# Head-compact recurrent weights: the key side as two 64-row matmuls per product, into two PSUM banks

## The chip, the core and the metric

The kernel runs on one core of one Trainium2 chip. TensorE (PE; its weight loads are shown as PEld) multiplies, VectorE (DVE), ScalarE (ACT) and GpSimd (POOL) do the elementwise work, SyncE (SP) moves tiles. The metric is the device time of one execution in microseconds. Everything is fp32. In the trace one fp32 matmul of the kernel shows as two PE instructions, one PE transpose as one.

## The reference, cut to what matters

The layer is a test-time-training attention over 2048 tokens, a windowed softmax attention and a mixture of experts with 32 experts, added to the input. The part that the change touches is the recurrence: four heads of size 64, 16 chunks of 128 tokens, and three weight matrices per head that change from chunk to chunk:

```
def step(carry, xi):
    W0, W1, W2, M0, M1, M2 = carry
    qi, ki, vi, l0, l1, l2, mi = xi
    hid = einsum('bcd,bhd->bch', qi, W2)
    gate = silu(einsum('bcd,bhd->bch', qi, W0))
    out = einsum('bch,boh->bco', gate * hid, W1)
    gba = einsum('bcd,bhd->bch', ki, W0)
    hbm = einsum('bcd,bhd->bch', ki, W2)
    sg = silu(gba); hidden = sg * hbm
    dhidden = einsum('bco,boh->bch', vi, W1)
    dhbm = dhidden * sg
    dgba = silu_bp(dhidden * hbm, gba)
    dw1 = einsum('bco,bch->boh', vi, hidden * l1)
    dw0 = einsum('bch,bcd->bhd', dgba, ki * l0)
    dw2 = einsum('bch,bcd->bhd', dhbm, ki * l2)
    # dw += momentum * mean; five Newton-Schulz steps; W = renorm(W + dw)
    ...
```

## The kernel before

The four heads are held as two groups (g = 0, 1) of two heads (h = 0, 1): head h of a group sits on partitions 64h to 64h+63. The 16 chunks are unrolled. Each of the 15 first chunks ends in a boundary, at which the weights of the next chunk become ready; the last chunk has no weight update.

Each engine runs one instruction list in an order written out by hand (`body` and its `fill` tables); semaphores join the lists. The pieces around the change are these.

- `renorm(m)` (DVE, L1175) writes the new weights `Wn[g]`, for group 0 and then group 1.
- `turn_w(m, g)` (PE, L736) turns `Wn[g]` with three PE transposes of 128 x 64 into `CA[g]`, on partitions 0 to 63. `w_T` (ACT) copies the result with two activations, one per head, into `WT[g]`, a 128 x 3 x 128 tile whose 64 x 64 blocks on the diagonal hold the turned weights of the two heads and whose other blocks stay zero.
- `w_bd(m)` (DVE, L1186 and L1187) copies the two blocks of W1 into the block-diagonal `W1BD[g]`: four copies of 64 x 64 for both groups, right behind `renorm`. Behind it stand `total`, `weights` and, in the next body, `ln_stats`.
- `k_side(i, g)` (PE) makes, for 128 tokens and both heads at once, one matmul of 256 moving columns against `WT` (W0 and W2) and one of 128 against `W1BD`, into one bank, `CB[g]`. ACT's `k_side` reads that bank (sigmoid of 128 columns, copy of 256 columns into `ks`), DVE's `k_side` (L1075 to L1094) makes the twelve elementwise steps of the gradient, POOL's `k_u` (L333) one product of it.
- `q_side(i)` (PE) makes four matmuls of 128 x 128 x 128 with `WT`, and `q_out(i)` two more with the W1 part of `WT`, which is block-diagonal.
- On DVE, `q_gate` (L1193, L1195) follows `k_side`, then `grad` (momentum, squares, row sums), then `sum_copy` and `x_first`. On PE, `grads(i, 0)` and `grads(i, 1)` wait for `dga`, then come `h_up(i, 2)`, half of `shared_up` (which waits for `gh` of `q_gate`), `sums` (waits for the row sums of `grad`), the other half of `shared_up`, `h_up(i, 3)` and the first turn of X (`ns_turn`, L699).
- On POOL, `k_u(i, 0)`, `k_u(i, 1)` and `h_sq(i, 1)` (L363, the square of 128 x 512) follow one another.

The names L426 (ACT) and L629 (PE matmul) are helper lines that many steps share; tiles tell them apart.

Of the kernel before, what the change touches and what calls it, by code (L numbers as in the profile page):

```python
# [27 lines left out]
ALU = mybir.AluOpType  # L28
ACT = mybir.ActivationFunctionType
# [3 lines left out]
P = 128  # L33
D = 256
KT = D // P
HD = 64
NH = 4
G = 2
# [9 lines left out]
W0, W2, W1 = range(3)  # L48
# [25 lines left out]
def build(nc, x, wall_d, rows_d, wo, fast_d, affine_d, fc1T, fc2T, e1T, e2T, upT, downT, ident_d, fixed_d, out):  # L74
# [3 lines left out]
    with ExitStack() as ctx:  # L78
        def sb(name, shape):
            return ctx.enter_context(nc.sbuf_tensor(name, shape, F32))  # L80

        def bank(name):
            return ctx.enter_context(nc.psum_tensor(name, [P, 512], F32))
# [13 lines left out]
        ident = sb("ident", [P, P])  # L97
# [10 lines left out]
        bias, gb, og_s = rows[:, 0:SMALL], rows[:, SMALL:SMALL + E], rows[:, SMALL + E:SMALL + E + HD]  # L108

        Wn = [sb(f"Wn{g}", [P, 3, HD]) for g in range(G)]  # L110
        W1BD = [sb(f"W1BD{g}", [P, P]) for g in range(G)]
        WT = [sb(f"WT{g}", [P, 3, P]) for g in range(G)]
        Mom = [sb(f"Mom{g}", [P, 3, HD]) for g in range(G)]
        nrm = [sb(f"nrm{g}", [P, 3]) for g in range(G)]

# [7 lines left out]
        ks = [sb(f"ks{g}", [P, 3, P]) for g in range(G)]  # L123
# [28 lines left out]
        vT = sb("vT", [P, G, P])  # L152
# [44 lines left out]
        CC = [ctx.enter_context(nc.psum_tensor(f"CC{g}", [P, 1024], F32)) for g in range(G)]  # L197
        CA = [CC[g][:, 0:512] for g in range(G)]
        CB = [CC[g][:, 512:1024] for g in range(G)]
        M0 = bank("M0")  # L200
        M1 = bank("M1")
        HB = bank("HB")
# [3 lines left out]
        def per_group(name):  # L206
            return [sem(f"{name}{g}") for g in range(G)]
# [13 lines left out]
        e_dw, e_G, e_s3, e_ssb, e_sst, e_pw, e_x = (per_group(n) for n in ("dw", "G", "s3", "ssb", "sst", "pw", "X"))  # L221
        e_ax, e_t, e_xt, e_am = (per_group(n) for n in ("aX", "turn", "XT", "Am"))
        e_prod, e_mp = (per_group(n) for n in ("product", "Mp"))
        e_up, e_rn, e_rp, e_wn, e_bd, e_wt, e_WT = (per_group(n) for n in ("upd", "rn", "rp", "Wn", "W1BD", "wt", "WT"))
        e_qs, e_gsig, e_gt1, e_gh, e_qo, e_to = (sem(n) for n in ("q_side", "gate_sig", "gt1", "gh", "q_out", "to_copied"))
        e_msq, e_rms, e_tf, e_ttt = (sem(n) for n in ("ms", "rms", "ttt_steps", "ttt_ready"))
        e_at, e_aT, e_win, e_as, e_sm, e_nb, e_pr = (sem(n) for n in ("raw_turned", "aT", "window", "scores", "masked", "negmax", "probs"))
# [187 lines left out]
        def _(act):  # L415
# [9 lines left out]
            def a(out_, in_, func, **kw):  # L425
                return nc.scalar.activation(out_, in_, func, **kw)  # L426
# [43 lines left out]

            def k_side(i, g):
                act.wait_ge(e_k[g], i + 1)
                a(ks[g][:, 0, :], CB[g][:, 0:P], ACT.Sigmoid)
                a(ks[g][:, 1:3, :].rearrange("p w c -> p (w c)"), CB[g][:, P:3 * P], ACT.Copy).then_inc(e_kc[g], 1)

            def xt(i, g, it):
                act.wait_ge(e_t[g], NI * i + it + 1)
# [2 lines left out]
            def w_T(m, g):  # L480

                act.wait_ge(e_wt[g], m + 1)
                for h in range(2):
                    c = slice(h * HD, (h + 1) * HD)
                    ins = a(WT[g][c, :, c], CA[g][0:HD, 0:3 * P].rearrange("p (w c) -> p w c", w=3)[:, :, c], ACT.Copy)
                ins.then_inc(e_WT[g], 1)

            def gate_sig(i):
                act.wait_ge(e_qs, i + 1)
# [127 lines left out]
        def _(pe):  # L617
# [10 lines left out]
            def mm(out_, lhsT, rhs, start=True, stop=True):  # L628
                return pe.matmul(out_, lhsT, rhs, start=start, stop=stop)  # L629
# [43 lines left out]
            def k_side(i, g):  # L673

                pe.wait_ge(e_qkT, i + 1)
                pe.wait_ge(e_vT, i + 1)
                pe.wait_ge(e_WT[g], i + 1)
                mm(CB[g][:, 0:2 * P], qkT[:, 2 + g, :], WT[g][:, W0:W2 + 1, :].rearrange("p w c -> p (w c)"))
                pe.wait_ge(e_bd[g], i + 1)
                mm(CB[g][:, 2 * P:3 * P], vT[:, g, :], W1BD[g][:, :]).then_inc(e_k[g], 1)  # L680

            def grads(i, g):
                if g == 0:
# [42 lines left out]
            def turn_w(m, g):  # L726

                if isinstance(m, int):
                    if m == 0:
                        pe.wait_ge(e_ttw, 16 * G)  # L730
                    else:
                        pe.wait_ge(e_wn[g], m)
                else:
                    wn_in[g].wait()
                for w in range(3):
                    ins = pe.transpose(CA[g][0:HD, w * P:(w + 1) * P], Wn[g][:, w, :], ident[:, :])  # L736
                ins.then_inc(e_wt[g], 1)


            def q_side(i):  # L740

                pe.wait_ge(e_ot, i)
                for g in range(G):
                    pe.wait_ge(e_WT[g], i + 1)
                pe.wait_ge(e_qkT, i + 1)
                for g in range(G):
                    for n, w in enumerate((W0, W2)):
                        ins = mm(M0[:, (2 * g + n) * P:(2 * g + n + 1) * P], WT[g][:, w, :], qkT[:, g, :])
                ins.then_inc(e_qs, 1)

            def q_out(i):
                pe.wait_ge(e_gh, i + 1)
                pe.wait_ge(e_aT, i + 1)
                for g in range(G):
                    ins = mm(M1[:, g * P:(g + 1) * P], gh[:, g, :], WT[g][:, W1, :])
                ins.then_inc(e_qo, 1)


# [209 lines left out]
        def _(dve):  # L968
# [7 lines left out]
            nc.vector.memset(vw[:, 1, :], 0.0)  # L976
            for g in range(G):
                nc.vector.memset(Mom[g][:, :, :], 0.0)
                nc.vector.memset(W1BD[g][:, :], 0.0)
                nc.vector.memset(WT[g][:, :, :], 0.0)  # L980
            nc.vector.memset(lt[:, :, :], 0.0).then_inc(e_init, 1)

            aggr_in = Expect(dve, e_stats, "aggr_in")
# [83 lines left out]
            def k_side(i):  # L1067


                tt, stt = nc.vector.tensor_tensor, nc.vector.scalar_tensor_tensor  # L1070
                sg, hbm, dhi = ([ks[g][:, n, :] for g in range(G)] for n in range(3))

                def silu(g):
                    dve.wait_ge(e_kc[g], i + 1)
                    tt(kt[g][:, 0, :], CB[g][:, 0:P], sg[g], ALU.mult).then_inc(e_kd[g], 1)  # L1075

                def slope(g):
                    dve.wait_ge(e_kd[g], 3 * i + 1)
                    stt(kt[g][:, 1, :], sg[g], 1.0, kt[g][:, 0, :], ALU.subtract, ALU.mult).then_inc(e_kd[g], 1)

                def derivative(g):
                    dve.wait_ge(e_kd[g], 3 * i + 2)
                    tt(kt[g][:, 2, :], sg[g], kt[g][:, 1, :], ALU.subtract).then_inc(e_kd[g], 1)

                def through(g):
                    dve.wait_ge(e_kd[g], 3 * i + 3)
                    dve.wait_ge(e_ku[g], i + 1)
                    tt(dga[g][:, :], kt[g][:, 2, :], kt[g][:, 3, :], ALU.mult).then_inc(e_dgr[g], 1)

                def hidden(g):  # L1090
                    tt(hid[g][:, :], kt[g][:, 0, :], hbm[g], ALU.mult)

                def dhidden(g):
                    tt(dhb[g][:, :], kt[g][:, 0, :], dhi[g], ALU.mult)  # L1094

                for step, g in ((silu, 0), (slope, 0), (hidden, 0), (silu, 1), (derivative, 0), (dhidden, 0), (slope, 1),
                                (through, 0), (hidden, 1), (derivative, 1), (dhidden, 1), (through, 1)):
                    step(g)
# [77 lines left out]
                                                      nrm[g][:, w:w + 1], ALU.mult, ALU.mult)  # L1176
                    ins.then_inc(e_wn[g], 1)

            def w_bd(m):

                for g in range(G):
                    if isinstance(m, int) and m == 0:
                        dve.wait_ge(e_ttw, 16 * G)
                    else:
                        dve.wait_ge(e_wn[g], m)
                    nc.vector.tensor_copy(W1BD[g][0:HD, 0:HD], Wn[g][0:HD, W1, :])  # L1186
                    nc.vector.tensor_copy(W1BD[g][HD:P, HD:P], Wn[g][HD:P, W1, :]).then_inc(e_bd[g], 1)  # L1187


            def q_gate(i):  # L1190
                dve.wait_ge(e_gsig, i + 1)
                v = M0[:, :].rearrange("p (g w t) -> p g w t", g=G, w=2)
                nc.vector.tensor_tensor(gt1[:, :, :], v[:, :, 0, :], gsig[:, :, :], ALU.mult).then_inc(e_gt1, 1)  # L1193
                dve.wait_ge(e_gt1, i + 1)
                nc.vector.tensor_tensor(gh[:, :, :], v[:, :, 1, :], gt1[:, :, :], ALU.mult).then_inc(e_gh, 1)  # L1195
# [146 lines left out]

            def body(i, last):
                if last:
                    q_gate(i)
                    att_scale(i)
                    y_acc(i, 1)
                    q_ms(i)
                    y_acc(i, 2)
                    att_mask(i)  # L1350
                    att_max(i)
                    y_acc(i, 3)
                    q_norm(i)
                    y_acc(i, 4)
                    att_out(i)
                    for u in range(5, NU):
                        y_acc(i, u)
                    y_sum(i)
                    total(i)
                    return  # L1360
                m = i + 1
                ln_stats(m)
                k_side(i)
                q_gate(i)
                grad(i)
                sum_copy(i, 0)
# [19 lines left out]
                update(i)  # L1386
                y_sum(i)
                renorm(m)
                w_bd(m)
                total(i)  # L1390
                weights(m)

# [6 lines left out]
            for g in range(G):  # L1399
                dve.wait_ge(e_rp[g], 1)  # L1400
                nc.vector.tensor_copy(nrm[g][:, :], r3[g][:, 4, :]).then_inc(e_up[g], 2)
            w_bd(0)
            dve.wait_ge(e_const, 16 * NCONST)
            prep_z(0)
            prep_silu_qk(0)
# [48 lines left out]
```

## Time and profile before

| | |
|---|---|
| median of 3 runs | 830.14 us (828.5 to 830.5) |
| profiled execution, its own time | 830.14 us |
| its span in the profile | 828.1 us |
| granted TensorE clock, mean | 0.996 of full speed |
| PE matmul busy | 780.7 us (94%) |
| DVE busy | 714.6 us (86%) |
| ACT busy | 354.0 us (43%) |
| POOL busy | 406.8 us (49%) |

The 2.0 us between the span and the execution's own time lie outside the profile. Busy shares are averages over the whole span. One chunk takes 51.34 us: the wait of POOL for the row sums at a boundary ends at 382.93 us in one chunk and at 434.27 us in the next, and the fifteen boundaries look alike. The boundary between 382 and 398 us of the span is the one read below.

### The profile page before, as it was taken

What the parts mean: (1) busy time and instruction counts of PE and PEld (TensorE: products, weight loads), DVE (VectorE), ACT (ScalarE), POOL (GpSimd) and SP (SyncE); (2) the same over time, 40 slices, a digit from 0 to 9 for tenths busy, and PEclk for the clock granted to TensorE, in tenths of its full rate; (3) what the DMA queues carried; (4) which work ended last, traced back from release to release, by engine and by line L of the source; (5) the groups of instructions that cost most, each with busy time, mean ns of one, the idle gap of its engine ahead of it and who ended that gap; (6) DMA issues with size and microseconds to landing.
All of it is one profiled execution on the core that took longest, in us unless ns stands there. A gap on an engine that the chain in (4) does not pass through costs nothing.

```text
span 828.1 us, 24889 instructions
## 1 busy us (share of the span) xinstructions
PE 780.7 (94%) x9776; PEld 668.5 (81%) x9776; DVE 714.6 (86%) x2592; ACT 354.0 (43%) x868; POOL 406.8 (49%) x535
## 2 busy tenths in 40 slices
PE   3899999999999999999999999999999999999997
PEld 1888888888888888878888788887888888888886
DVE  4789898898988979889798897988979889898876
ACT  2544344443444434444344444444444444434533
POOL 1654555445454454544555445544465444655442
PEclk9899999999999999999999999999999999999999
DMA  8100000000000000000000000000000000000000
GB/s 321 54 3 14 9 2 21 3 13 9 2 21 2 14 8 2 21 2 15 8 3 20 2 15 9 3 21 2 15 8 2 21 2 15 8 2 15 2 15 7
DMA packets 9811, 15.09 MB, mean 18 GB/s; under 512 B 1120, under 2 KB 8928, under 8 KB 9440
## 3 DMA queue, kind: packets, MB, share of 16 engines
q1 hardware_dynamic: 7904, 7.80, 3.2%
q10 hardware_dynamic: 1792, 5.70, 1.8%
q8 instruction: 78, 1.28, 0.6%
q14 instruction: 37, 0.30, 0.1%
HBM read 11.41 MB, written 2.10 MB: 16 GB/s over the span
## 4 chain that ended last, share of the span: by engine, by line
PE 53%; DVE 33%; issue 6%; ACT 5%; POOL 2%; DMA 1%; SPq 0%; DVEq 0%
PE CC L629 18%; PE M L629 13%; PE HB L629 8%; DVE acc L1328 8%; PE YB L629 8%; DVE Wn L1175 4%; DVE Mp L1138 2%; DVE dhb L1094 2%; DVE X L1146 2%; PE CC L699 2%; DVE Am L1131 2%; POOL r L285 2%; DVE sm L1233 1%; DMA rows<-in_rows 1%; PE CC L700 1%
## 5 line engine op out<-in xcount | busy, mean ns | idle before, releaser
L363 POOL TENSOR_TENSOR hq<-hr 128x512 f32<-128x512 f32 x128 | 137.1, 1071 | 71.9 <-ACT hr L426 71.9
L285 POOL TENSOR_TENSOR r<-r,half 128x3 f32<-128x3 f32 (+1 forms) x78 | 77.9, 1011 | 155.1 <-DVE r L1116 67.9
L629 PE MATMUL HB<-xlT,e_s 128*128 128x128 f32 x1024 | 143.0, 283 | 0.4 <-ACT xlT L426 0.4
L629 PE MATMUL YB<-e_s,hq 128*128 128x128 f32 x1024 | 141.3, 281 | 1.8 <-DVE acc L1328 0.8
L629 PEld LDWEIGHTS HB<-xlT,e_s 128*128 128x128 f32 x1024 | 126.7, 193 | 6.8 <-ACT xlT L426 0.7
L1328 DVE SCALAR_TENSOR_TENSOR acc<-YB,cw,acc 128x128 f32<-128x128 f32 x448 | 125.4, 342 | 7.9 <-PE YB L629 7.9
L341 POOL TENSOR_TENSOR aX<-X,a_tile 128x192 f32<-128x192 f32 x150 | 92.9, 640 | 79.9 <-DVE X L1146 79.9
L426 ACT ACTIVATE hr<-HB 128x512 f32<-128x512 f32 x128 | 76.1, 594 | 128.5 <-PE HB L629 128.5
L629 PEld LDWEIGHTS YB<-e_s,hq 128*128 128x128 f32 x1024 | 124.2, 191 | 7.4 <-issue 4.1
L629 PEld LDWEIGHTS CC<-X,Mp 64*64 64x64 f32 x1800 | 58.3, 135 | 23.6 <-issue 11.3
L629 PEld LDWEIGHTS CC<-Am 64*64 64x64 f32 x1800 | 59.5, 134 | 21.8 <-DVE Am L1131 18.2
L426 ACT ACTIVATE XT<-CC 128x256 f32<-128x256 f32 x150 | 50.8, 381 | 59.7 <-PE CC L700 59.5
L629 PE MATMUL CC<-X,Mp 64*64 64x64 f32 x1800 | 68.6, 222 | 7.6 <-DVE Mp L1138 7.6
L629 PE MATMUL CC<-Am 64*64 64x64 f32 x1800 | 69.8, 223 | 1.9
L1146 DVE SCALAR_TENSOR_TENSOR X<-CC,aX 128x192 f32<-128x192 f32 x150 | 51.3, 352 | 13.4 <-PE CC L629 13.3
L629 PE MATMUL M<-wall,xnT 128*128 128x512 f32 (+1 forms) x128 | 56.9, 551 | 3.6 <-DMA rows<-in_rows 3.6
L629 PEld LDWEIGHTS CC<-XT 64*64 64x64 f32 x1800 | 43.2, 133 | 20.7 <-ACT XT L426 14.7
L1131 DVE COPY Am<-CC 128x192 f32<-128x192 f32 x150 | 48.4, 347 | 9.3 <-PE CC L629 8.3
L1138 DVE SCALAR_TENSOR_TENSOR Mp<-Am,CC 128x192 f32<-128x192 f32 x150 | 49.8, 351 | 7.2 <-PE CC L629 3.6
L629 PE MATMUL CC<-XT 64*64 64x64 f32 x1800 | 55.6, 232 | 0.0
L699 PE MATMUL CC<-ident,X 128*64 128x128 f32 x150 | 39.7, 281 | 0.0
L333 POOL TENSOR_TENSOR kt<-ks 128x128 f32<-128x128 f32 x30 | 13.7, 459 | 51.0 <-ACT ks L426 51.0
(180 smaller groups left out, 1525.3 us busy)
## 6 DMA issues: line engine op xcount, KB each, us to landing
xa<-in_x SPq DMA_DIRECT2D x16, 128.0 KB, 2.1
e_s<-in_e1T ACTq DMA_DIRECT2D x1, 2048.0 KB, 12.7
e_s<-in_e2T ACTq DMA_DIRECT2D x1, 2048.0 KB, 19.3
xr<-in_x SPq DMA_DIRECT2D x16, 128.0 KB, 2.2
out<-ot SPq DMA_DIRECT2D x16, 128.0 KB, 1.7
wall<-in_wall SPq DMA_DIRECT2D x1, 820.0 KB, 7.1
up_s<-in_upT ACTq DMA_DIRECT2D x1, 512.0 KB, 15.9
down_s<-in_downT ACTq DMA_DIRECT2D x1, 512.0 KB, 20.0
```

Of the source, the lines that this page charges most:

```text
L285: return pool.tensor_tensor(dst, src, expo[:, 0:n], ALU.pow)
L341: pool.tensor_tensor(aX[g][:, :, :].rearrange("p w c -> p (w c)"), X[g][:, :, :].rearrange("p w c -> p (w c)"), a_tile[:, it, :], ALU.mult ...
L363: pool.tensor_tensor(hq[b][:, :, :], hr[b][:, :, :], hr[b][:, :, :], ALU.mult).then_inc(e_hq, 1)
L426: return nc.scalar.activation(out_, in_, func, **kw)
L629: return pe.matmul(out_, lhsT, rhs, start=start, stop=stop)
L699: pe.transpose(CA[g][0:HD, 0:P], X[g][:, 0, :], ident[:, :])
L1094: tt(dhb[g][:, :], kt[g][:, 0, :], dhi[g], ALU.mult)
L1131: nc.vector.tensor_copy(Am[g][:, :, :], CC[g][:, 0:6 * P].rearrange("p (w c) -> p w c", w=3)[:, :, 0:HD])\
L1138: nc.vector.scalar_tensor_tensor(Mp[g][:, :, :].rearrange("p w c -> p (w c)"), Am[g][:, :, :].rearrange("p w c -> p (w c)"), b / c, CA[g][ ...
L1146: nc.vector.scalar_tensor_tensor(X[g][:, :, :].rearrange("p w c -> p (w c)"), CB[g][:, 0:3 * HD], NS[it][2], aX[g][:, :, :].rearrange("p w ...
L1175: ins = nc.vector.tensor_scalar(Wn[g][:, w, :], Wn[g][:, w, :], r3[g][:, 5, w:w + 1], nrm[g][:, w:w + 1], ALU.mult, ALU.mult)
L1328: ins = nc.vector.scalar_tensor_tensor(acc[:, e, :], y, w, acc[:, e, :], ALU.mult, ALU.add)
```

## The change

The turned weights are kept compact: `WT[g]` becomes 128 x 3 x 64, head h on its own 64 partitions, without zeros.

- `turn_w` makes six matmuls of 64 x 64 x 64 against the identity, each on its head's partitions, in place of three transposes. `w_T` becomes one activation of 128 x 192.
- `k_side` on PE makes, per head, one matmul with 64 rows of contraction and 128 moving columns (W0 and W2), head 0 into `CA[g]` and head 1 into `CB[g]`, and then one per head with 64 moving columns for W1, which it takes straight from `Wn`. `KS[g]` is a view of both banks, through which ACT's and DVE's steps read.
- `q_side` makes eight matmuls of 64 x 64 with 128 moving columns in place of four full ones.
- `w_bd` is gone. A new `w_out(i)` on DVE writes the block-diagonal `WO[g]` (for `q_out`) from `WT`, with four copies of the same shape; it stands behind DVE's `k_side` and before `q_gate`.
- At the start the memsets of `W1BD` and of `WT` (two of 128 x 384) are replaced by one of `WO` per group.

```diff
         Wn = [sb(f"Wn{g}", [P, 3, HD]) for g in range(G)]
-        W1BD = [sb(f"W1BD{g}", [P, P]) for g in range(G)]
-        WT = [sb(f"WT{g}", [P, 3, P]) for g in range(G)]
+        WT = [sb(f"WT{g}", [P, 3, HD]) for g in range(G)]
+        WO = [sb(f"WO{g}", [P, P]) for g in range(G)]
...
+        KS = [CC[g][:, :].rearrange("p (h c) -> p h c", h=2)[:, :, 0:3 * HD] for g in range(G)]
...
             def k_side(i, g):
                 act.wait_ge(e_k[g], i + 1)
-                a(ks[g][:, 0, :], CB[g][:, 0:P], ACT.Sigmoid)
-                a(ks[g][:, 1:3, :].rearrange("p w c -> p (w c)"), CB[g][:, P:3 * P], ACT.Copy).then_inc(e_kc[g], 1)
+                a(ks[g][:, 0, :].rearrange("p (h c) -> p h c", h=2), KS[g][:, :, 0:HD], ACT.Sigmoid)
+                a(ks[g][:, 1:3, :].rearrange("p w (h c) -> p h w c", h=2),
+                  KS[g][:, :, HD:3 * HD].rearrange("p h (w c) -> p h w c", w=2), ACT.Copy).then_inc(e_kc[g], 1)
...
                 act.wait_ge(e_wt[g], m + 1)
-                for h in range(2):
-                    c = slice(h * HD, (h + 1) * HD)
-                    ins = a(WT[g][c, :, c], CA[g][0:HD, 0:3 * P].rearrange("p (w c) -> p w c", w=3)[:, :, c], ACT.Copy)
-                ins.then_inc(e_WT[g], 1)
+                a(WT[g][:, :, :].rearrange("p w c -> p (w c)"), CA[g][:, 0:3 * HD], ACT.Copy).then_inc(e_WT[g], 1)
...
                 pe.wait_ge(e_WT[g], i + 1)
-                mm(CB[g][:, 0:2 * P], qkT[:, 2 + g, :], WT[g][:, W0:W2 + 1, :].rearrange("p w c -> p (w c)"))
-                pe.wait_ge(e_bd[g], i + 1)
-                mm(CB[g][:, 2 * P:3 * P], vT[:, g, :], W1BD[g][:, :]).then_inc(e_k[g], 1)
+                halves = [(slice(h * HD, (h + 1) * HD), (CA, CB)[h][g]) for h in range(2)]
+                for c, dst in halves:
+                    mm(dst[:, 0:2 * HD], qkT[c, 2 + g, :], WT[g][c, W0:W2 + 1, :].rearrange("p w c -> p (w c)"))
+                for c, dst in halves:
+                    ins = mm(dst[:, 2 * HD:3 * HD], vT[c, g, :], Wn[g][c, W1, :])
+                ins.then_inc(e_k[g], 1)
...
                 for w in range(3):
-                    ins = pe.transpose(CA[g][0:HD, w * P:(w + 1) * P], Wn[g][:, w, :], ident[:, :])
+                    for h in range(2):
+                        c = slice(h * HD, (h + 1) * HD)
+                        ins = mm(CA[g][c, w * HD:(w + 1) * HD], Wn[g][c, w, :], ident[c, c])
                 ins.then_inc(e_wt[g], 1)
...
                     for n, w in enumerate((W0, W2)):
-                        ins = mm(M0[:, (2 * g + n) * P:(2 * g + n + 1) * P], WT[g][:, w, :], qkT[:, g, :])
+                        for h in range(2):
+                            c = slice(h * HD, (h + 1) * HD)
+                            ins = mm(M0[c, (2 * g + n) * P:(2 * g + n + 1) * P], WT[g][c, w, :], qkT[c, g, :])
...
-                    ins = mm(M1[:, g * P:(g + 1) * P], gh[:, g, :], WT[g][:, W1, :])
+                    pe.wait_ge(e_wo[g], i + 1)
+                    ins = mm(M1[:, g * P:(g + 1) * P], gh[:, g, :], WO[g][:, :])
...
-                nc.vector.memset(W1BD[g][:, :], 0.0)
-                nc.vector.memset(WT[g][:, :, :], 0.0)
+                nc.vector.memset(WO[g][:, :], 0.0)
...
-            def w_bd(m):
-
-                for g in range(G):
-                    if isinstance(m, int) and m == 0:
-                        dve.wait_ge(e_ttw, 16 * G)
-                    else:
-                        dve.wait_ge(e_wn[g], m)
-                    nc.vector.tensor_copy(W1BD[g][0:HD, 0:HD], Wn[g][0:HD, W1, :])
-                    nc.vector.tensor_copy(W1BD[g][HD:P, HD:P], Wn[g][HD:P, W1, :]).then_inc(e_bd[g], 1)
+            def w_out(i):
+
+                for g in range(G):
+                    dve.wait_ge(e_WT[g], i + 1)
+                    nc.vector.tensor_copy(WO[g][0:HD, 0:HD], WT[g][0:HD, W1, :])
+                    nc.vector.tensor_copy(WO[g][HD:P, HD:P], WT[g][HD:P, W1, :]).then_inc(e_wo[g], 1)
...
                 if last:
+                    w_out(i)
                     q_gate(i)
...
                 k_side(i)
+                w_out(i)
                 q_gate(i)
...
                 renorm(m)
-                w_bd(m)
                 total(i)
```

## Rows read from the trace of the kernel before

**Rows 1.** The page: busy time by engine, shares of the chain by engine.
```profile
PE 780.7 (94%) x9776; PEld 668.5 (81%) x9776; DVE 714.6 (86%) x2592; ACT 354.0 (43%) x868; POOL 406.8 (49%) x535
...
PE 53%; DVE 33%; issue 6%; ACT 5%; POOL 2%; DMA 1%; SPq 0%; DVEq 0%
```
**Rows 2.** The chain at one boundary, in order of time: start, us, what.
```profile
388.20 0.91 PE CC L629 x4
389.13 0.56 ACT ks L426 x2
...
390.29 1.12 DVE dhb L1094
...
392.68 0.73 PE CC L629 x12
```
**Rows 3.** The timeline from the new weights to DVE's key side: start, us, engine, line, operation, [idle before, releaser].
```profile
386.71 0.18 DVE L1186 COPY W1BD<-Wn 64x64 f32<-64x64 f32 x1
386.85 0.52 PE L736 MATMUL CC<-ident,Wn 128*64 128x128 f32 x3
...
387.32 0.19 DVE L1187 COPY W1BD<-Wn 64x64 f32<-64x64 f32 x1
387.40 0.66 ACT L426 ACTIVATE WT<-CC 64x192 f32<-64x192 f32 x2 [0.43 <-PE CC L736]
...
387.63 0.39 PE L629 MATMUL CC<-W1BD,vT 128*128 128x128 f32 x2
...
388.77 0.28 DVE L1075 TENSOR_TENSOR kt<-CC,ks 128x128 f32<-128x128 f32 x1
```
**Rows 4.** The timeline from there to the first turn of X.
```profile
389.76 0.46 POOL L333 TENSOR_TENSOR kt<-ks 128x128 f32<-128x128 f32 x1 [0.59 <-ACT ks L426]
...
389.92 0.44 DVE L1083 TENSOR_TENSOR kt<-ks,kt 128x128 f32<-128x128 f32 x1
...
390.17 1.09 POOL L363 TENSOR_TENSOR hq<-hr 128x512 f32<-128x512 f32 x1
...
391.96 0.30 PE L629 MATMUL CC<-kl,dga 128*64 128x64 f32 x2 [0.64 <-DVE dga L1088]
...
392.34 0.28 DVE L1088 TENSOR_TENSOR dga<-kt 128x128 f32<-128x128 f32 x1
...
392.99 0.42 DVE L1195 TENSOR_TENSOR gh<-M,gt 128x256 f32<-128x256 f32 x1
...
393.33 0.73 DVE L1105 SCALAR_TENSOR_TENSOR Mom<-Mom,mmc,CC 128x192 f32<-128x192 f32 x2
...
394.51 0.60 DVE L1112 TENSOR_REDUCE r<-sq 128x3 f32<-128x192 f32 x2
...
395.12 0.53 PEld L629 LDWEIGHTS CC<-r,fixed 128*128 128x128 f32 x4
...
397.08 0.36 DVE L1126 TENSOR_TENSOR X<-Mom,r 128x192 f32<-128x192 f32 x1
...
397.50 0.30 PE L699 MATMUL CC<-ident,X 128*64 128x128 f32 x1
```
**Rows 5.** Timeline rows of runs of weight loads and matmuls of either size.
```profile
394.22 0.97 PEld L629 LDWEIGHTS M<-xnT,up_s 128*128 128x128 f32 x8
```
```profile
398.95 0.32 PEld L629 LDWEIGHTS CC<-XT 64*64 64x64 f32 x12 [0.17 <-issue]
398.95 0.46 PE L629 MATMUL CC<-XT 64*64 64x64 f32 x12
```
```profile
407.59 0.78 PEld L629 LDWEIGHTS CC<-Am 64*64 64x64 f32 x24 [0.76 <-DVE Am L1131]
```
**Rows 6.** Groups by line and shape, ACT: xcount | busy us, mean ns | idle before.
```profile
L426 ACT ACTIVATE XT<-CC 128x256 f32<-128x256 f32 x150 | 50.8, 381 | 59.7 <-PE CC L700 59.5
...
L426 ACT ACTIVATE ks<-CC 128x128 f32<-128x128 f32 x30 | 8.3, 278 | 7.3 <-PE CC L629 6.9
```
**Rows 7.** The timeline at the start of the program.
```profile
12.09 5.08 PE L629 MATMUL M<-wall,xnT 128*128 128x512 f32 x8 [3.60 <-DMA rows<-in_rows]
```

More of the change, by code:

```diff
@@ L223, in build @@
         e_prod, e_mp = (per_group(n) for n in ("product", "Mp"))
-        e_up, e_rn, e_rp, e_wn, e_bd, e_wt, e_WT = (per_group(n) for n in ("upd", "rn", "rp", "Wn", "W1BD", "wt", "WT"))
+        e_up, e_rn, e_rp, e_wn, e_wo, e_wt, e_WT = (per_group(n) for n in ("upd", "rn", "rp", "Wn", "WO", "wt", "WT"))
         e_qs, e_gsig, e_gt1, e_gh, e_qo, e_to = (sem(n) for n in ("q_side", "gate_sig", "gt1", "gh", "q_out", "to_copied"))
@@ L1074, in silu @@
                     dve.wait_ge(e_kc[g], i + 1)
-                    tt(kt[g][:, 0, :], CB[g][:, 0:P], sg[g], ALU.mult).then_inc(e_kd[g], 1)
+                    tt(kt[g][:, 0, :].rearrange("p (h c) -> p h c", h=2), KS[g][:, :, 0:HD],
+                       sg[g].rearrange("p (h c) -> p h c", h=2), ALU.mult).then_inc(e_kd[g], 1)
                 def slope(g):
@@ L1401, in _ @@
                 nc.vector.tensor_copy(nrm[g][:, :], r3[g][:, 4, :]).then_inc(e_up[g], 2)
-            w_bd(0)
             dve.wait_ge(e_const, 16 * NCONST)
```

## The prediction, made before the changed kernel was run

> **What bounds the kernel now.** I read the page first: PE has 94% matmul busy time and the chain lies 53% on PE and 33% on DVE [rows 1]. So neither engine alone sets the time; they hand a chain to each other, and what counts is which of them is late at each hand-over around the edit. The second view was the chain in order of time at one of the 15 boundaries [rows 2], the third the timeline of all engines over the same stretch [rows 3, 4]. The reader should see four hand-overs.
>
> (a) The weights of group 1 are complete just before PE's turn of them starts, at 386.85; it ends at 387.37, ACT copies them with two activations until 388.06, PE makes `k_side` of group 1 from 388.20 to 389.11, ACT's two activations take 0.56 [rows 2, 3]. So `ks` of group 1 is there at 389.69. The four copies of `w_bd` run beside this on DVE, and DVE's first step on group 0 starts at 388.77 [rows 3].
>
> (b) The next wait is between DVE and POOL. `k_u` of group 1 on POOL starts at 389.76, and `h_sq` behind it ends at 391.26. DVE's `dhb`, a step of the same shape as `dga` (0.28), takes 1.12 and ends at 391.41, 0.15 behind POOL [rows 2, 4]. The derivative step L1083 (0.44) got through between the two POOL instructions.
>
> (c) From there DVE works without a gap: last `dga` at 392.34, ends 392.62; `q_gate` until 393.41 (`gh`: 392.99 + 0.42); momentum, squares and row sums until 395.11 [rows 4]. PE makes `grads(1)` at 392.68, right behind `dga`.
>
> (d) `sums` starts on PE at 395.12. Its data of group 0 was there at 394.87 (the first of the two reductions of 394.51 to 395.11; I read 0.24 back for the second). PE is here the later one, by 0.25. Then X of group 0 is ready at 397.44 and PE turns it at 397.50 [rows 4]: both arrive together, so a delay of `sums` goes through to the Newton-Schulz steps in full.
>
> **The change part by part**, for one boundary.
>
> *Turn.* Three transposes of 0.52 in all [rows 3] become six matmuls, 12 instructions of 64 x 64 x 64. Twelve such instructions take 0.46 from first start to last end [rows 5]. The end moves by -0.06: from 387.37 to 387.31.
>
> *Copy of the turned weights.* Two activations, 0.66 [rows 3], become one of 128 x 192. Between 278 ns for 128 columns and 381 for 256 [rows 6] that is 0.33. `WT` of group 1 is ready at 387.31 + 0.02 + 0.33 = 387.66 instead of 388.06.
>
> *Key side on PE.* Before, a group has 2 instructions of 256 columns and 2 of 128; now 8 instructions with 64 rows: 4 with 128 moving columns and 4 with 64, all with 128 weight columns. The trace has no instruction of 64 rows by 128 columns. The nearest rows give two bounds. If the row halves work side by side as the 64 x 64 quarters do, I scale from these: 12 loads start within 0.32 and 24 within 0.78, so 0.024 to 0.030 each at 64 columns, 0.05 to 0.06 at 128 [rows 5]. If they don't, each costs what a full 128-column load costs, 0.97/8 = 0.12 less overlap, so 0.11 (the next step of PE after these eight loads is 0.90 later) [rows 5]. I take 0.06, since the 64 x 64 products alternate the halves in just this way. Group 0 starts at about 387.25: last start 387.25 + 7 x 0.06 = 387.67, with some 0.23 for the last matmul itself 387.90. Before, its last matmul ended at 387.63 + 0.39 = 388.02 [rows 3]. Group 1 follows without waiting for `WT`, and ends about 388.45, before ACT is done with group 0. ACT then sets the time: `ks` of group 0 at 387.90 + 0.57 = 388.47, of group 1 at 389.04. That is 0.65 earlier than 389.69. I cost the strided reads of the two banks by ACT and DVE at nothing, since the element counts are the same; if each lost 0.05 by it, the gain below would be 0.1 less, which the range holds.
>
> The Trainium skill (TensorE: Matmul & The Clock Gate, section LDWEIGHTS) says that a weight load takes a time given by its columns, whatever its rows, which speaks against halving the rows: eight loads of 128 columns for four. Its section on packing small matmuls says that loads for different row groups overlap with running matmuls. With the first alone the sum would be the rival B below, with both it is my forecast; the trace agrees with the second for 64 x 64 shapes [rows 5] and shows no 64 x 128 shape.
>
> *What DVE makes of the 0.65.* The gain can't pass (b) whole. `h_sq` now ends at about 391.26 - 0.65 = 390.61, but DVE comes to its derivative step, the fifth instruction behind `ks` of group 0, at 388.47 + 4 x 0.28 = 389.6 at the earliest, and at 390.0 if one of the four waits for a `k_u` (0.46). If it reaches the gap between `k_u` and `h_sq` as before, only `dhb` waits, and all is gained: 0.54 to 0.65. If it misses it, the derivative waits behind `h_sq` too, which costs one more step of 0.20 (the pitch of these steps), and leaves about 0.40. I take g = 0.45 for the gain at the last `dga`.
>
> The Trainium skill (SBUF — State Buffer, who interferes with whom) calls this an exclusive lock on a shared pair of ports, taken for a whole instruction. The trace agrees: `dhb` ends 0.15 behind POOL's instruction [rows 4].
>
> *w_bd leaves, w_out comes.* The four copies cost 0.80 at 386.71 to 387.51 [rows 3]. There they are covered: DVE waits for `ks` anyway, so taking them out gives at most the 0.14 by which DVE's first step was later than `ks` of group 0. In the new place, between the last `dga` and `q_gate`, nothing covers them: DVE is busy without a gap from (b) to the row sums. I charge 0.80. Queued behind are `q_gate`, momentum, squares and row sums, and `sums` on PE waits for the last. `gh` would come at 393.41 + 0.80 - g; PE wants it for `shared_up` at 394.22 - g [rows 4, 5], so that wait just doesn't open. PE's `sums` could run at 395.12 - g, its data comes at 394.87 + 0.80 - g. PE waits 0.55. What is left of each boundary is
>
> shift = 0.80 - 0.25 - g = 0.55 - g = +0.10 us.
>
> *q_side.* Eight instructions of 128 x 128 with 128 columns become 16 of 64 x 64 with 128 moving columns. By the pitches above, 16 x 0.055 = 0.9, as before; serial it would be 1.8. PE stands idle for 0.64 before `grads` [rows 4] and comes free up to 0.6 sooner from `k_side`, so even the high bound costs nothing there. `q_out` has the same matmuls and a wait that is long over.
>
> *Start and end.* The memsets and the four copies before the first chunk (some 1.5 us of DVE) lie before 12.09 us, when PE's projection has waited 3.60 us for a DMA [rows 7]: nothing. In the last chunk there is no key side: `w_out` needs only `WT`, and DVE then waits for PE's `q_side` and ACT's gate, so it is covered; uncovered it would cost 0.80 once.
>
> *The sum.* 15 x 0.10 = +1.5 us on the profiled execution's own 830.14, which is also the median: 831.6. With g between 0.40 and 0.65, +2.3 to -1.5.
>
> **The rivals.**
>
> A, the forecast: the halves overlap, the moved copies use up what that gives. 831.6, own range 828.6 to 834.5.
>
> B: the row halves don't overlap. Pitch 0.11: group 0 ends at 387.25 + 0.77 + 0.22 = 388.24, group 1 at 389.12, `ks` of group 1 at 389.69 as before, g = 0. Shift 0.55, +8.3 us: 838.4. For it: eight full-width loads where there were four. Against it: the 64 x 64 rows.
>
> C, faster: the shared port is passed at the best moment and DVE's first step is freed of its 0.14 too. g = 0.65 + 0.14 = 0.79, shift -0.24, -3.6 us: 826.5. It decides as soon as g exceeds 0.55 + 0.17 = 0.72. Against it: DVE would have to find the port free at each of its steps.
>
> D, the port takes more: with `ks` of group 1 close behind that of group 0, POOL's two `k_u` and `h_sq` stand back to back, and two or three DVE steps wait instead of one. g = 0.20, shift 0.35, +5.3 us: 835.4. For it: DVE's step L1083 already stretches to 0.44 behind `k_u` [rows 4].
>
> **How the numbers follow.** A 0.52 (of which 0.46 within 0.3%, that is 2.5 us, about what a measurement of this kernel can tell from no change, and 0.06 above), B 0.18, C 0.12, D 0.18. Faster 0.12, same 0.46, slower 0.42. The prediction is A's. The range from 826.5 to 838.5 holds A, D, C's value and B's at its edge; half of B and half of C may lie outside, 0.15.
>
> **What would show it.** ACT copies `WT` in one piece of 0.33 and starts `ks` of group 1 right behind that of group 0; weight loads of 64 x 128 at a pitch near 0.06; DVE's copies between `dga` and `gt`, 0.80; PE idle for about 0.5 before `sums`, with DVE's reduction as releaser, where it had none. The chunk of 51.34 us becomes 51.4. Wrong would be: loads at 0.11 (B), a `dga` that comes less than 0.3 sooner after the weights (D), no wait before `sums` (C). What would upset all of it is a moved phase between POOL and DVE somewhere in the Newton-Schulz steps, which I assume to keep their pattern.

## The result, and the profile of the changed kernel

The changed kernel takes 834.52 us (median of 5 runs, 833.24 to 834.67) against 830.25 us (5 runs) of the kernel before: 0.51% slower, ratio 1.0051, interval 1.0037 to 1.0066. That is inside the predicted range, 2.9 us above its point of 831.6 and at the upper edge of the narrower range that the prediction gave its own forecast (828.6 to 834.5). The profiled execution took 833.24 us, the shortest of the five, with a span of 831.3.

The page, busy time and the chain by engine. The columns are those of [rows 1].

```profile
PE 789.5 (95%) x10312; PEld 672.7 (81%) x10312; DVE 714.5 (86%) x2590; ACT 344.2 (41%) x836; POOL 408.6 (49%) x535
...
PE 48%; DVE 39%; issue 6%; ACT 4%; POOL 2%; DMA 1%; SPq 0%; DVEq 0%
```

VectorE is as busy as before (714.5 against 714.6 us). Yet its share of the chain rose from 33% to 39%, and PE's fell from 53% to 48%. The same amount of VectorE work now stands in a place where something waits for it; the lines below show which.

The chain at the same boundary, with the wait that ends each chunk's weight update as a clock.

```profile
383.83 0.86 POOL r L286
...
389.00 0.56 ACT ks L427 x2
...
390.82 1.12 DVE dhb L1101
...
393.92 0.44 DVE gt L1197
...
394.38 0.42 DVE gh L1199
394.80 0.65 DVE Mom L1112 x2
...
396.30 0.64 PE CC L628 x4
...
435.45 0.86 POOL r L286
```

This view gives the loss. A chunk takes 435.45 - 383.83 = 51.62 us, where it took 51.34: 0.28 more, and 15 x 0.28 = 4.2 us. The medians differ by 4.27. Before, the chain went from the last `dga` to PE's `grads`; now it stays on VectorE through the gate, momentum and squares. POOL's step starts at 383.83 where it started at 382.93, so 0.90 is taken off the times below to lay them beside [rows 3, 4].

The timeline of the boundary.

```profile
386.94 0.76 DVE L1182 TENSOR_SCALAR Wn<-Wn,r,nrm 128x64 f32<-128x64 f32 x3
...
387.79 0.43 PEld L628 LDWEIGHTS CC<-ident,Wn 64*64 64x64 f32 x12 [0.33 <-DVE Wn L1182]
387.80 0.56 PE L628 MATMUL CC<-ident,Wn 64*64 64x64 f32 x12
...
388.29 0.30 PEld L628 LDWEIGHTS CC<-WT,qkT 64*128 64x128 f32 x4
388.29 0.49 PE L628 MATMUL CC<-WT,qkT 64*128 64x128 f32 x4
...
388.41 0.33 ACT L427 ACTIVATE WT<-CC 128x192 f32<-128x192 f32 x1 [0.79 <-PE CC L628]
388.51 0.31 PEld L628 LDWEIGHTS CC<-Wn,vT 64*128 64x128 f32 x4
388.62 0.34 PE L628 MATMUL CC<-Wn,vT 64*128 64x64 f32 x4
...
388.85 0.33 PEld L628 LDWEIGHTS CC<-WT,qkT 64*128 64x128 f32 x4
388.88 0.49 PE L628 MATMUL CC<-WT,qkT 64*128 64x128 f32 x4
389.00 1.13 ACT L427 ACTIVATE ks<-CC 128x128 f32<-128x128 f32 x4 [0.26 <-PE CC L628]
...
390.56 0.34 DVE L1090 TENSOR_TENSOR kt<-ks,kt 128x128 f32<-128x128 f32 x1
...
390.71 1.09 POOL L364 TENSOR_TENSOR hq<-hr 128x512 f32<-128x512 f32 x1
...
392.50 0.30 PE L628 MATMUL CC<-kl,dga 128*64 128x64 f32 x2 [0.45 <-DVE dga L1095]
...
392.88 0.27 DVE L1095 TENSOR_TENSOR dga<-kt 128x128 f32<-128x128 f32 x1
...
393.08 0.18 DVE L1190 COPY WO<-WT 64x64 f32<-64x64 f32 x1
...
393.70 0.19 DVE L1191 COPY WO<-WT 64x64 f32<-64x64 f32 x1
...
394.87 1.15 PE L628 MATMUL M<-xnT,up_s 128*128 128x128 f32 x8
...
395.91 0.60 DVE L1119 TENSOR_REDUCE r<-sq 128x3 f32<-128x192 f32 x2
...
396.30 0.64 PE L628 MATMUL CC<-r,fixed 128*128 128x3 f32 x4 [0.29 <-DVE r L1119]
...
398.27 0.36 DVE L1133 TENSOR_TENSOR X<-Mom,r 128x192 f32<-128x192 f32 x1
```

The reader should see three things. First, ACT now runs all four activations of `ks` in one piece, 389.00 to 390.13; less 0.90 that ends at 389.23, where it ended at 389.69: 0.46 gained. Second, the last `dga` starts at 391.98 on the old clock, where it started at 392.34: 0.36 of the 0.46 is left. Third, the four copies follow it, and the reductions start at 395.01 on the old clock instead of 394.51: 0.50 late. PE's `sums` says in its bracket that it sat idle for 0.29 until VectorE's reduction. No such wait stood at that place before. X follows, 398.27 - 0.90 = 397.37 against 397.08 [rows 4]: 0.29 late. So 0.21 of the 0.50 was covered.

The start of the program went the other way. PE's projection of the first chunk began earlier:

```profile
10.40 4.29 PE L628 MATMUL M<-wall,xnT 128*128 128x512 f32 x5 [2.52 <-DMA rows<-in_rows]
```

It was 12.09 before [rows 7]. After seven boundaries of +0.28 the clock should be 1.96 late and is only 0.90 late. About 0.6 of that 1.1 us was gained at the start: the last `dga` of the first chunk starts at 31.62 instead of 32.56, which is 0.94 sooner, and 0.36 of this is the gain that every boundary has. Another 0.35 belongs to the kernel before, in whose profiled execution one early chunk took 51.69 us and the others 51.33 to 51.36; the rest is rounding of the 0.28. The profiled execution is also the shortest of its five. Whether the change has part in the earlier start was not tried.

### The profile page after: what moved, and what is told of

It is laid out like the page before. It is cut to its first block, busy times and chain, and to the rows that moved or that the text cites. A ratio compares the mean times of both kernels' runs of the same rounds, so it can differ in the third digit from the quotient of the medians.

```text
span 831.3 us, 25927 instructions
## 1 busy us (share of the span) xinstructions
PE 789.5 (95%) x10312; PEld 672.7 (81%) x10312; DVE 714.5 (86%) x2590; ACT 344.2 (41%) x836; POOL 408.6 (49%) x535
## 4 chain that ended last, share of the span: by engine, by line
PE 48%; DVE 39%; issue 6%; ACT 4%; POOL 2%; DMA 1%; SPq 0%; DVEq 0%
PE CC L628 17%; PE M L628 13%; DVE acc L1332 8%; PE YB L628 8%; PE HB L628 6%; DVE Wn L1182 3%; DVE dhb L1101 2%; DVE Mp L1145 2%; DVE X L1153 2%; PE CC L701 2%; DVE Am L1138 2%; POOL r L286 2%; DVE sm L1237 1%; PE CC L702 1%; DVE r L1243 1%
## 5 line engine op out<-in xcount | busy, mean ns | idle before, releaser
L702 PE MATMUL CC<-ident,X 128*128 128x128 f32 x150 | 38.5, 273 | 0.0
```

The source lines that it names most:

```text
L702: pe.transpose(CA[g][:, P:2 * P], X[g][:, 1:3, :].rearrange("p w c -> p (w c)"), ident[:, :])\
```

## The experiments

Every time is a median, with the ratio to the kernel before, which was run beside it on the same chip (830.99 us for the first four, 830.79 for the last four). The recorded expectations speak of theories. Theory 1: the moved copies stand on a stretch of VectorE without a gap. Theory 2: the added PE instructions are the cost. Theory 3: GpSimd's instruction holds up VectorE's `dhb`. Theory 4: the row halves overlap only where neighbouring instructions use different halves.

**The copies on another engine.** From the changed kernel:

```diff
+            def w_out(i):            # on ScalarE
+                for g in range(G):
+                    act.wait_ge(e_WT[g], i + 1)
+                    a(WO[g][0:HD, 0:HD], WT[g][0:HD, W1, :], ACT.Copy)
+                    a(WO[g][HD:P, HD:P], WT[g][HD:P, W1, :], ACT.Copy).then_inc(e_wo[g], 1)
...
                 gate_sig(i)
+                w_out(i)
                 y_first(i)
...
                 k_side(i)            # on VectorE
-                w_out(i)
                 q_gate(i)
```

> The changed kernel with the four copies of w_out taken off VectorE: ScalarE makes them, behind gate_sig and before y_first, where it waits 1.09 us for PE. Theory 1 (the copies stand on VectorE's gapless stretch before the row sums): every boundary loses the 0.28 us that it got longer and keeps the 0.36 us by which the last dga now comes sooner, 15 x 0.64 = 9.6 us off 834.5, so about 825. PE's sums then have no wait on VectorE's reduction. Theory 2 (the added PE instructions are the cost: 12 for 3 in each turn, 16 for 8 in q_side): 833 to 835, no change.

825.1 us, ratio 0.9932 (0.9920 to 0.9945). The timeline at one boundary:

```profile
337.06 1.05 ACT L427 ACTIVATE WO<-WT 64x64 f32<-64x64 f32 x4
...
338.25 1.14 ACT L427 ACTIVATE acc<-YB,cw 128x128 f32<-128x128 f32 x4
...
339.04 0.28 DVE L1103 TENSOR_TENSOR dga<-kt 128x128 f32<-128x128 f32 x1
...
339.25 0.41 DVE L1205 TENSOR_TENSOR gt<-M,gsig 128x256 f32<-128x256 f32 x1
```

ScalarE fits the four copies (1.05) in ahead of `acc`, and the gate follows the last `dga` after 0.21 again. The chunk by the same clock:

```profile
330.00 0.86 POOL r L286
...
381.00 0.86 POOL r L286
```

51.00 us, 0.62 less than with the change, 0.34 less than before. All the added PE instructions are still in this kernel, so they are not the cost, and theory 2 falls.

**The same four copies in the kernel before,** at the place where `w_out` stands, into a tile that nobody reads:

```diff
                 k_side(i)
+                for g in range(G):
+                    nc.vector.tensor_copy(spare[g][0:HD, 0:HD], WT[g][0:HD, W1, 0:HD])
+                    nc.vector.tensor_copy(spare[g][HD:P, HD:P], WT[g][HD:P, W1, HD:P])
                 q_gate(i)
```

> The kernel before, nothing taken out, with four more copies of 64 x 64 from WT into a spare tile, standing where w_out stands in the changed kernel; nobody reads them. Theory 1: 0.80 to 0.83 us more on VectorE less the 0.20 to 0.25 us by which PE was late there, 15 x 0.6 = 9 us more than before, so 839. Theory 2: the place is harmless, under 1.5 us more (831).

839.54 us, ratio 1.0106 (1.0090 to 1.0121), as theory 1 said. The clock:

```profile
333.54 0.86 POOL r L286
...
385.50 0.86 POOL r L286
```

51.96 us, 0.62 more than before (the medians differ by 8.5 us, a little less than 15 x 0.62). Taking the copies away gives 0.62 and putting them in costs 0.62, in two kernels with different key sides.

**The copies behind `grad`.** From the changed kernel:

```diff
                 k_side(i)
-                w_out(i)
                 q_gate(i)
                 grad(i)
+                w_out(i)
```

> The changed kernel with w_out on VectorE moved from before q_gate to behind grad, so before sum_copy, where VectorE waits for PE's sums in any case (0.22 us with the change, 0.43 before). Theory 1: gate, momentum and row sums come 0.83 us sooner, sum_copy is then late by the 0.4 us of the copies that the wait does not cover, net 0.0 to 0.1 us a boundary against the kernel before: 830.5 to 832. Theory 2: 834 to 835.

830.0 us, ratio 0.9984 (0.9975 to 0.9993): a little below the expected 830.5 to 832, and on theory 1's side. The timeline:

```profile
342.99 0.17 DVE L1190 COPY WO<-WT 64x64 f32<-64x64 f32 x1
343.07 0.53 PEld L628 LDWEIGHTS CC<-r,fixed 128*128 128x128 f32 x4
...
343.60 0.19 DVE L1191 COPY WO<-WT 64x64 f32<-64x64 f32 x1
343.83 0.23 DVE L1123 COPY r<-CC 128x3 f32<-128x3 f32 x2
```

The copies now run beside PE's `sums`, which hides about half of them. VectorE's reductions end at 343.07 and `sum_copy` starts 0.76 later, right behind the last copy; before, it started 0.44 after them, so some 0.32 of the 0.80 is left uncovered. A better place on VectorE alone takes the whole loss away.

**GpSimd's square out of the way.** From the first kernel of this section:

```diff
                 k_u(i, 1)
+                pool.wait_ge(e_dgr[1], i + 1)
                 h_sq(i, 1)
```

> The first kernel of this set (copies on ScalarE), and GpSimd's h_sq(i, 1) made to wait for the last dga of VectorE's key side, so that its 1.1 us no longer lies beside VectorE's steps with two SBUF inputs. Theory 3 (the stretched dhb of 1.12 us is GpSimd holding a port): dhb takes 0.28, the last dga comes 0.8 us sooner, PE then has no idle time left before grads (0.45 us of it goes), so 15 x 0.45 = 7 us less than the first kernel, about 818. Rival: dhb is slow for a reason of its own or the wait only moves the collision to the squares: no faster than the first kernel, 825 or more.

812.47 us, ratio 0.9781 (0.9767 to 0.9794), a larger gain than the expected 818. The timeline:

```profile
332.00 0.28 DVE L1110 TENSOR_TENSOR dhb<-kt,ks 128x128 f32<-128x128 f32 x1
...
333.21 0.28 DVE L1104 TENSOR_TENSOR dga<-kt 128x128 f32<-128x128 f32 x1
...
333.57 1.04 POOL L364 TENSOR_TENSOR hq<-hr 128x512 f32<-128x512 f32 x1 [1.64 <-DVE dga L1104]
```

`dhb` takes 0.28 where it took 1.12, with the same operands, once `hq` isn't beside it; this holds for all 30 instructions of `dhb`, of which 15 took 1.12 before. A chunk takes 50.15 us, 0.85 less than the kernel it was made from, and PE's waits for `dga`, 7.5 us in total in that kernel, shrink to 0.2. My 0.45 counted the idle time of PE's matmuls before the first `grads` alone. In the first kernel of this section PE's weight loads stood idle longer there, and again between the two `grads`:

```profile
338.63 0.19 PEld L636 LDWEIGHTS CC<-kl,dga 128*64 128x64 f32 x2 [0.61 <-issue]
...
339.37 0.19 PEld L636 LDWEIGHTS CC<-kl,dga 128*64 128x64 f32 x2 [0.15 <-DVE dga L1103]
```

Together that is 0.76 of the 0.85; where the other 0.09 comes from was not traced.

**That wait alone, in the kernel before:**

```diff
                 k_u(i, 1)
+                pool.wait_ge(e_dgr[1], i + 1)
                 h_sq(i, 1)
```

> The kernel before, with one wait added: GpSimd's h_sq(i, 1) waits for the last dga. Theory 3 (GpSimd's instruction holds VectorE's dhb up): the gain does not depend on the compact weights. dhb falls to 0.28, the last dga comes 0.8 us sooner, PE loses its 0.64 us of idle time before grads and the 0.15 us between the two grads: 15 x 0.8 = 12 us less than the kernel before, 818 to 820. Rival: without the earlier key side PE isn't free, and the gain is under half of it: 824 or more.

819.75 us, ratio 0.9861 (0.9849 to 0.9874), as theory 3 said. The held-up `dhb` is a cost of the kernel before too, and no part of the change.

**The order of the halves.** From the kernel with both edits above (812.47 us):

```diff
                 for c, dst in halves:
                     mm(dst[:, 0:2 * HD], qkT[c, 2 + g, :], WT[g][c, W0:W2 + 1, :]...)
-                for c, dst in halves:
                     ins = mm(dst[:, 2 * HD:3 * HD], vT[c, g, :], Wn[g][c, W1, :])
```

> The fourth kernel of the first set (copies on ScalarE, h_sq late), with PE's key side in another order: both products of head 0, then both of head 1, in place of the heads alternating. Theory 4 (the row halves overlap only where neighbouring instructions use different halves): the pitch rises from 0.07 to near 0.11 within a head, 0.2 to 0.3 us later per group, 3 to 6 us more than 812.5. Rival (PE takes instructions of the other half out of order, or the 0.07 is an issue limit and no overlap): within 1 us of 812.5.

811.89 us, ratio 0.9782 (0.9767 to 0.9796): no difference. Theory 4's expectation was wrong. The timeline of group 0:

```profile
328.76 0.31 PEld L637 LDWEIGHTS CC<-WT,qkT 64*128 64x128 f32 x4
...
328.97 0.31 PEld L637 LDWEIGHTS CC<-Wn,vT 64*128 64x128 f32 x4
```

Although the program now has both products of head 0 first, the four loads from `WT`, of both heads, all come first: the last of them ends after 0.31, and as each lasts 0.18 to 0.19, they start within 0.12. The first load of `Wn` starts after 0.21, as in the changed kernel. So by these rows PE starts work for the second head ahead of the first head's second product, against program order.

**The key side alone.** From the kernel before, with the ACT and DVE readers of the changed kernel:

```diff
-                mm(CB[g][:, 0:2 * P], qkT[:, 2 + g, :], WT[g][:, W0:W2 + 1, :].rearrange("p w c -> p (w c)"))
-                pe.wait_ge(e_bd[g], i + 1)
-                mm(CB[g][:, 2 * P:3 * P], vT[:, g, :], W1BD[g][:, :]).then_inc(e_k[g], 1)
+                halves = [(slice(h * HD, (h + 1) * HD), (CA, CB)[h][g]) for h in range(2)]
+                for c, dst in halves:
+                    mm(dst[:, 0:2 * HD].rearrange("p (w c) -> p w c", w=2), qkT[c, 2 + g, :], WT[g][c, W0:W2 + 1, c])
+                for c, dst in halves:
+                    ins = mm(dst[:, 2 * HD:3 * HD], vT[c, g, :], Wn[g][c, W1, :])
+                ins.then_inc(e_k[g], 1)
...
-                w_bd(m)
```

> One part of the change alone: the kernel before (WT block-diagonal, turn by transposes, w_T by two activations, q_side and q_out full), with only the key side on the two row halves in two banks and read through both, W1 taken from Wn, w_bd gone and no w_out anywhere. Theory 1: the key side is what brings ks of group 1 0.46 us sooner; turn and w_T add nothing to it, since ScalarE waits for nothing but PE and itself: 825, as the first kernel. Rival: the single w_T and the matmul turn are needed for it, and ks of group 1 comes 0.1 to 0.2 us sooner only: 828 to 830.

827.44 us, ratio 0.9955 (0.9942 to 0.9968): between the theory (825) and its rival (828 to 830). The timeline shows what the theory left out and the rival named:

```profile
334.10 0.66 ACT L427 ACTIVATE WT<-CC 64x192 f32<-64x192 f32 x2 [0.42 <-PE CC L741]
...
334.79 0.55 ACT L427 ACTIVATE ks<-CC 128x128 f32<-128x128 f32 x2
...
334.91 0.49 PE L631 MATMUL CC<-WT,qkT 64*128 64x128 f32 x4 [0.25 <-ACT WT L427]
...
335.61 0.55 ACT L427 ACTIVATE ks<-CC 128x128 f32<-128x128 f32 x2 [0.27 <-PE CC L631]
```

With two activations `WT` of group 1 comes late, PE waits 0.25 for it, and ACT 0.27 for PE. `ks` of group 1 is complete 2.61 us after the turn of group 1 starts (336.16 against 333.55), where it was 2.84 before and is 2.33 in the changed kernel: about half the gain. A chunk takes 51.13 us, against 51.00 in the first kernel of this section. The single activation is the likely difference, by these waits, but the turn and `q_side` differ too, and none was tried alone.

**The key side alone, and the wait:**

> The kernel before with the key side on row halves alone (as above), and h_sq(i, 1) waiting for the last dga. Theories 1 and 3 together: 812 to 813, as the fourth kernel of the first set, with 8 small PE instructions fewer per turn. Rival: the second transposing form or ScalarE's two w_T bind once the port is free: 815 or more.

816.37 us, ratio 0.9824 (0.9811 to 0.9837): the rival was right. This is 816.37 - 812.47 = 3.9 us more than with the rest of the change, but not all of it belongs to the compact weights. A chunk takes 50.28 us against 50.14 (between the last `dga` of one chunk and of the next), which is 2.1 us over fifteen. Most of the rest lies behind the last `dga`, which takes 77.98 us against 76.17, and there the granted clock differs in the two profiled executions:

```profile
775.00:790.00 15.00, 13.12 (x102) 11.82 (x101) 10.20 (x33) 5.48 (x15) 4.18 (x5) 0.89 0.06 19
```
```profile
773.00:788.00 15.00, 13.68 (x144) 12.32 (x144) 10.13 (x33) 6.31 (x18) 5.15 (x6) 1.00 0.06 19
```

The third number from the end is the granted clock: 0.89 in this kernel and 1.00 in the other, at the same place of the last chunk. TensorE's clock fell here from 2.4 to 1.2 GHz for part of it, after PE had stood idle twice, for 0.86 and 0.95 us. In the other kernel it stood idle there for 0.61 and 0.63 and kept its clock; so it did in the kernel before, with 0.85 and 0.95. The kernel before with the one wait added shows the fall again, and 77.97 us behind its last `dga` where the kernel before has 76.33, though the edit touches nothing there. So about 2 us of the 3.9 are shown to come from the rest of the change, and whether it has part in the clock is open.

The fastest kernel here is the changed one with the copies on ScalarE and the square held back: 812 us, 2.2% below the kernel before.

## Why the prediction was nearly right, point by point

The mechanism held: a gain on the key side, eaten by copies that were moved from a covered place to an uncovered one. The outcome, +0.28 a boundary, lies between the forecast A (+0.10) and the rival D (+0.35), and nearer to D's number, though D's mechanism did not come. I gave the largest chance, 0.46, to "within 0.3%" and 0.42 to slower, and 0.51% slower is what came. What was off is the size of terms:

| term, us per boundary | forecast | measured |
|---|---|---|
| the four copies, in line | 0.80 | 0.85 or 0.86 |
| cover: PE later than its data at `sums` | 0.25 | 0.21 |
| `ks` of group 1 sooner | 0.65 | 0.46 |
| of which the last `dga` sooner, g | 0.45 | 0.36 |
| shift | 0.10 | 0.28 |

The 0.18 between the two shifts is half the smaller g (0.09) and half the copies (0.05) and their cover (0.04). The g itself came out close partly by luck. `ks` was 0.19 less early than forecast, and the wait on GpSimd swallowed 0.10 of it where I had let it swallow 0.20.

*Turn.* Of the 0.19 on `ks` most was lost here. I said that twelve 64 x 64 instructions take 0.46, so the turn ends 0.06 sooner. They took 0.56, and began 0.10 after the weights instead of 0.06: the turn ends 0.09 later (388.36 - 0.90 = 387.46 against 387.37). I took the wrong row. The 0.46 belongs to `CC<-XT`, a product that uses all four quarters of the array; the turn uses the two on the diagonal, as `CC<-Am` does. That row was in front of me: 24 loads in 0.78, one of them 0.14, so 0.028 apart [rows 5]. The turn's loads are (0.43 - 0.14)/11 = 0.026 apart, those of `XT` (0.32 - 0.14)/11 = 0.016. (The prediction read 0.32 as the time within which the loads start; it runs to the end of the last, and they start within 0.18.) PE also pauses between the two shapes: from the last load of the turn (387.79 + 0.43 - 0.14 = 388.08) to the first of the key side (388.29) there is 0.20, where the kernel before has 0.11 between its transposes and its key side. So the key side of group 0 starts at 388.29 - 0.90 = 387.39, for the forecast 387.25.

*Copy of the turned weights.* 0.33, as forecast.

*Key side on PE.* I took 0.06 between the bounds of 0.05 and 0.11, as the average from one instruction to the next. Group 0 has its eight loads between 388.29 and 388.51 + 0.31 = 388.82; the last lasts 0.19, so they start within 0.34, which is 0.05 apart. The halves do work side by side, and the window from 388.2 to 388.3 shows how:

```profile
388.29 0.38 PE L628 MATMUL CC<-WT,qkT 64*128 64x128 f32 x2
```

Two matmuls of 0.37 each fit in 0.38: they start 0.007 apart, one for either half by the program. The next pair of loads follows 0.11 later, the step of a full-width load. Rival B is out. Group 0 ran 388.29 to 388.96, which is 0.67 for the expected 0.65. One assumption was wrong and cost nothing: group 1 does wait for `WT`, whose activation ends at 388.74; its first load starts 0.11 later, at 388.85, as it did before (388.06 and 388.17). ScalarE is still busy with group 0 then. The last 0.04 of the 0.19 is the hand-over to ScalarE (388.96 to 389.00), which I had left out.

*The port.* `ks` was 0.46 sooner and the last `dga` 0.36. The derivative step (0.34) again passed between `k_u` and `h_sq`, and only `dhb` waited; rival D's mechanism, two or three steps held up, did not come. The direct test held GpSimd's instruction back and `dhb` fell from 1.12 to 0.28, so it is shown that this instruction is the cause.

*The moved copies.* The time from the last `dga` to the start of `gh` rose from 0.65 (392.99 - 392.34) to 1.50 (394.38 - 392.88): 0.85. Reductions 0.50 late, plus 0.36, gives 0.86. PE's wait before `sums` opened, 0.29 on its matmuls for the 0.55 that I had said; part of the difference is that PE's `shared_up` came later too, at 394.87, just behind the end of `gh` at 394.80. I had that wait as just not opening.

*What I costed at nothing.* The first kernel of the experiments has `q_side` on quarters and the strided reads, and is 0.34 a boundary faster than the kernel before, close to the 0.36 that the last `dga` gained. So behind that `dga` at most some 0.02 is left for them; what they cost ahead of it is inside the 0.36. `q_side` took more than the 0.9 I gave it: from its first load, at 389.47, to the next step of PE, at 390.49, is 1.02, where it was 0.89 (388.82 to 389.71). PE then still waited 0.45 for `dga`, so this was covered, as forecast.

## What to carry to other kernels

Before moving an instruction, ask of the new place what you ask of an edit: who waits behind it, and is that engine ever idle between there and the next hand-over. Here four copies of 0.19 us were covered in one place, but for 0.14 us at most, and cost 9 us in all in another, while the engine's busy share stayed the same. Price tiled matmuls from a row that uses the same parts of the array, not only the same shape, and add what the engine loses between one shape and the next. And where one elementwise instruction takes four times its usual time, look at what the neighbour engine runs beside it: one wait there was worth more than the whole change.

## What the runs showed of the hardware that was not expected

- Matmuls of 64 rows by 128 columns on the two row halves, into two PSUM banks, start in pairs: 0.007 us within a pair, and the loads of the next pair 0.11 later, which is what one full load takes. The order of the halves in the program made no difference (811.89 against 812.47 us).
- Twelve 64 x 64 fp32 matmul instructions take 0.56 us on two diagonal quarters, and 0.46 on four. No run changed the quarters alone.
- VectorE's multiply of two SBUF tiles, 0.28 us, took 1.12 beside GpSimd's multiply of 128 x 512, in each of the 15 boundaries of both kernels. The Trainium skill (SBUF — State Buffer, Who interferes with whom) calls it an exclusive lock; the 1.12 and the 0.28 without the neighbour agree.
- The Trainium skill (TensorEngine Tiling (Array Packing), Key Properties) says that a change of tiling mode drains the array. The trace shows a pause at each such change in the changed kernel: 0.20 us between the last load of 64 x 64 and the first of 64 x 128, in all 14 places where one follows the other, and 0.26 the other way, in all 15, where loads of one shape that wait for nothing follow at 0.11 or less. That the array is empty in between is not shown: the first 64 x 128 matmul starts at 388.29 and the last of the 64 x 64 ends at 387.80 + 0.56 = 388.36, but the profile models the ends.
